# Two-layer graph kernel on one core: two transposes moved from TensorE to transposing DMA transfers

## The reference, cut to what matters

```python
h = relu(layernorm(x))
q, k, v = h @ Wq + bq, h @ Wk + bk, h @ Wv + bv
a = q @ k.T / sqrt(512)
a = a * adj + (1 - adj) * -1e6          # adj[src, dst] = 1 for each edge
x = x + softmax(a) @ v                  # x1 in the kernel
h = relu(layernorm(x))                  # h2
h = agg(h @ W1 + b1)                    # agg: product with the edge counts, scaled by dinv on both sides
h = relu(gamma * (h - mean) * rsqrt(var + eps) + beta)   # over the nodes
return x + agg(h @ W2 + b2)
```

## Time and profile before

| | before |
|---|---|
| median of 3 runs | 340.11 us (339.83 to 340.81) |
| the profiled execution's own time | 340.02 us |
| its span, first to last instruction | 338.2 us |
| PE busy | 320.2 us, 95% |
| DVE busy | 200.9 us, 59% |
| ACT busy | 112.9 us, 33% |
| POOL busy | 54.6 us, 16% |
| granted TensorE clock, mean | 1.00 |

### The profile page before, as it was taken

How to read it: one execution, slowest core, us unless ns; L and a number is a source line. 1 busy time by engine, 2 the same in 40 slices (tenths; PEclk the granted TensorE clock), 3 DMA queues, 4 the chain that set the end, 5 groups by cost and what they waited for, 6 DMA issues and landing times.

```text
span 338.2 us, 4827 instructions
## 1 busy us (share of the span) xinstructions
PE 320.2 (95%) x1466; PEld 247.5 (73%) x1466; DVE 200.9 (59%) x456; ACT 112.9 (33%) x183; POOL 54.6 (16%) x96
## 2 busy tenths in 40 slices
PE   1898889999999999899999999999999999999996
PEld 0776456777666687788888888888778887887884
DVE  5889999986869514346263636446541257559221
ACT  1909123443464412422342322232621205514000
POOL 5113000000000081512306150120101014300000
PEclk9999999999999999999999999999999999999999
DMA  7912100000230060140202030000000000000041
GB/s 217 320 39 64 62 0 1 3 0 23 102 125 0 2 124 0 36 151 1 64 1 62 2 93 0 2 0 0 0 3 0 0 2 1 2 0 0 28 150 73
DMA packets 17477, 14.83 MB, mean 44 GB/s; under 512 B 11184, under 2 KB 11440, under 8 KB 17456
## 3 DMA queue, kind: packets, MB, share of 16 engines
q1 hardware_dynamic: 17456, 14.56, 14.4%
HBM read 10.36 MB, written 2.10 MB: 37 GB/s over the span
## 4 chain that ended last, share of the span: by engine, by line
PE 78%; DVE 10%; ACT 5%; issue 3%; DVEq 1%; POOL 1%; DMA 1%; SPq 0%; ACTq 0%; POOLq 0%
PE ps L787 17%; PE ps L789 16%; PE ps L788 16%; PE ps L1065 9%; PE ps L850 8%; PE ps L984 5%; PE ps L868 3%; PE ps L927 2%; DVE src_oh L606 2%; PE ps L816 1%; ACT cnt L458 1%; PE ps L948 1%; DMA edge_i<-src_in 1%; DVE bnst L756 1%; DVE g L753 1%
## 5 line engine op out<-in xcount | busy, mean ns | idle before, releaser
L606 DVE TENSOR_SCALAR src_oh<-iota,ecol 128x512 f16 x172 | 48.9, 349 | 1.7 <-PE ps L850 0.9
L850 PE MATMUL ps<-src_oh,dst_oh 128*128 x172 | 41.2, 381 | 2.0 <-DVE dst_oh L608 2.0
L389 ACT ACTIVATE cnt<-ps 64x512 int16<-64x512 f32 x32 | 18.9, 591 | 37.8 <-PE ps L855 37.4
L850 PEld LDWEIGHTS ps<-src_oh,dst_oh 128*128 x172 | 18.3, 114 | 17.8 <-issue 5.5
L984 PE MATMUL ps<-cnt,qh 128*128 128x512 f32 x128 | 30.1, 391 | 0.2 <-ACT cnt L458 0.2
L1065 PE MATMUL ps<-qh,cnt 128*128 128x512 f32 x128 | 29.3, 390 | 0.0
L984 PEld LDWEIGHTS ps<-cnt,qh 128*128 128x128 f32 x128 | 23.9, 188 | 5.5 <-issue 0.6
L1065 PEld LDWEIGHTS ps<-qh,cnt 128*128 128x128 f32 x128 | 23.9, 188 | 5.2 <-DVE vb L768 0.3
L787 PE MATMUL ps<-v,pT 128*128 128x512 f32 x64 | 25.0, 391 | 1.0 <-DVE pT L667 1.0
L787 PE MATMUL ps<-kT,qh 128*128 128x512 f32 x64 | 25.4, 397 | 0.0
L686 DVE TENSOR_TENSOR hnT<-ps,hnT 128x512 fp32r<-128x512 f32 x8 | 5.5, 692 | 33.2 <-ACT hnT L450 33.2
(11 more groups left out here) (150 smaller groups left out, 614.0 us busy)
## 6 DMA issues: line engine op xcount, KB each, us to landing
xt<-x_in SPq DMA_DIRECT2D x16, 256.0 KB, 3.1
out<-xt SPq DMA_DIRECT2D x8, 256.0 KB, 2.0
wA_raw<-L_gnn_Wk_in SPq DMA_DIRECT2D x2, 512.0 KB, 6.6
wB_raw<-L_gnn_Wv_in SPq DMA_DIRECT2D x2, 512.0 KB, 8.1
wA_raw<-L_gnn_Wq_in SPq DMA_DIRECT2D x2, 512.0 KB, 3.7
wB_raw<-L_gnn_W_in SPq DMA_DIRECT2D x2, 512.0 KB, 3.8
w_raw<-L_gnn_W_in SPq DMA_DIRECT2D x2, 512.0 KB, 3.8
bias_row<-L_gnn_b_in SPq DMA_DIRECT2D x2, 256.0 KB, 3.7
```

The source lines that it names most:

```text
L389: act.activation(cnt16[rows, a * KC:(a + 1) * KC, w // 2, :], ps[a * WIN:(a + 1) * WIN, i % 2, :].rearrange("p (s n) -> p s n", n=P), ACT. ...
L606: dve.tensor_scalar(src_oh[:, bass.ds(slot, 1), j, :].rearrange("p a n -> p (a n)"), iota[:, :], ecol[:, bass.ds(c + j, 1)], None, ALU.is_ ...
L850: m = pe.matmul(ps[:, i % 2, :], dst_oh[:, bass.ds(slot, 1), :, j].rearrange("p a n -> p (a n)"), src_oh[:, bass.ds(slot, 1), j, :].rearra ...
```

## The change

P and h2 are no longer turned on PE. ACT scales the values by a power of two and writes the rounded fp16 value (plane 0), DVE writes the fp16 rest (plane 1), SP issues one transposing DMA for each plane, and ACT and DVE turn the landed planes back into the fp32r pair. PSUM banks 5 and 6 are free of P; `weighted_v` uses bank 4. pT, p16 and h16 have one buffer each. `ADJ` falls from 4 to 2, so `turn_counts(t+2)` waits for mask t.

The orders change with it: on PE `weighted_v(i-1)` stands ahead of `times_w1(i-2)`, also at the tail; on DVE `mask_and_max(0)` stands ahead of the query split and `large_flag`; on SP all transfers of the pipeline stand in one loop.

```diff
-ADJ = 4
+ADJ = 2
+P_UNIT = 32768.0
+H_UNIT = 2048.0
@@ SP
+        def turn_p(t, part, split, done, landed):
+            sp.wait_ge(S[split], t + 1)
+            if t >= 1:
+                sp.wait_ge(S[done], t)
+            sp.dma_start_transpose(p16T[:, part, :, :], p16[:, part, :]).then_inc(S[landed], 16)
...
-        sp.wait_ge(S["item_ps"], len(items))
-        load_w(4)
-        for t in range(XT, NT):
-            load_x(NT + t)
-            if t >= 4:
-                turn_counts(t)
+        for t in range(NT + 2):
+            if t < NT:
+                turn_p(t, 0, "p16_hi", "p_hi", "p16_hi_in")
+                turn_p(t, 1, "p16_lo", "p_lo", "p16_lo_in")
+            if 1 <= t <= NT:
+                turn_h2(t - 1, 0, "h16_hi", "h2T_hi", "h16_hi_in")
+                turn_h2(t - 1, 1, "h16_lo", "h2T_lo", "h16_lo_in")
+            if t == 0:
+                sp.wait_ge(S["item_ps"], len(items))
+                load_w(4)
+            if t + ADJ < NT:
+                turn_counts(t + ADJ)
+            if XT <= t + 3 < NT:
+                load_x(NT + t + 3)
@@ POOL, mask_fill(t)
-                pool.wait_ge(S["pT_ps"], t - 1)
+                pool.wait_ge(S["p16_lo"], t - 1)
@@ ACT
+        def p16_hi(t):
+            act.wait_ge(S["exp_done"], t + 1)
+            if t >= 1:
+                act.wait_ge(S["p16_hi_in"], 16 * t)
+            act.activation(p16[:, 0, :], T[:, t % 2, :], ACT.Copy, scale=P_UNIT).then_inc(S["p16_hi"], 1)
         def p_hi(t):
-            act.wait_ge(S["pT_ps"], t + 1)
-            if t >= 2:
-                act.wait_ge(S["pv_ps"], t - 1)
-            act.activation(pT[:, t % 2, 0, :, :], ps[:, 4:6, :].rearrange("p a (k n) -> p (a k) n", n=P),
-                           ACT.Copy).then_inc(S["p_hi"], 1)
+            act.wait_ge(S["p16_hi_in"], 16 * (t + 1))
+            if t >= 1:
+                act.wait_ge(S["pv_ps"], t)
+            act.activation(pT[:, 0, :, :], p16T[:, 0, :, :], ACT.Copy, scale=1.0 / P_UNIT).then_inc(S["p_hi"], 1)
...
+        for i in range(NT + 3):
+            if 2 <= i <= NT + 1:
                 h2_relu(i - 2)
+                h16_hi(i - 2)
+            if 2 <= i <= NT:
+                p_hi(i - 1)
+            if i >= 3:
+                h1_hi(i - 3)
+            if 2 <= i <= NT + 1:
                 h2T_hi(i - 2)
+            if i < NT:
+                softmax_exp(i)
+            if i == 1:
+                act.wait_ge(S["hT_half_used"], 1)
+                p_hi(0)
+            if i < NT:
+                p16_hi(i)
@@ DVE
+        def p16_lo(t):
+            dve.wait_ge(S["p16_hi"], t + 1)
+            if t >= 1:
+                dve.wait_ge(S["p16_lo_in"], 16 * t)
+            dve.scalar_tensor_tensor(out=p16[:, 1, :], in0=T[:, t % 2, :], scalar=P_UNIT, in1=p16[:, 0, :], op0=ALU.mult,
+                                     op1=ALU.subtract).then_inc(S["p16_lo"], 1)
             dve.wait_ge(S["exp_done"], t + 1)
             dve.reciprocal(smx[:, 3, t:t + 1], smx[:, 2, t:t + 1]).then_inc(S["rinv_ready"], 1)
...
+        for i in range(NT + 3):
+            if 2 <= i <= NT + 1:
+                h16_lo(i - 2)
+            if 2 <= i <= NT:
+                p_lo(i - 1)
+            if i >= 3:
+                h1_tmp(i - 3)
+                h1_lo(i - 3)
+            if 2 <= i <= NT + 1:
+                h2T_lo(i - 2)
             if i < NT:
                 mask_and_max(i)
                 add_loops(i)
+            if i == 0:
+                large_flag()
+            if i == 1:
+                dve.wait_ge(S["hT_half_used"], 1)
+                p_lo(0)
+            if i < NT:
+                p16_lo(i)
...
             if i == NT - 1:
 ...
             if 1 <= i <= NT:
                 residual(i - 1)
@@ PE
-                    if (n, k) == (1, KC - 1) and t >= 2:
-                        h2_turn(t - 2)
...
-            if i >= 1:
-                p_turn(i - 1)
             if i == 1:
                 make(("q", 1, 2))
                 make(("q", 1, 3))
+            if i >= 1:
+                weighted_v(i - 1)
             if i >= 2:
                 times_w1(i - 2)
-            if i >= 1:
-                weighted_v(i - 1)
...
-        early = (0, 4, 1, 5, 2, 3)
+        early = (0, 4, 1, 2, 3, 5)
         agg1((0, 1), early)
-        h2_turn(NT - 2)
-        p_turn(NT - 1)
+        weighted_v(NT - 1)
         times_w1(NT - 2)
-        weighted_v(NT - 1)
         pe.wait_ge(S["masked"], NT)
         agg1((2, 3), early)
-        h2_turn(NT - 1)
+        pe.wait_ge(S["x1_ready"], NT)
```

More of the change, by code:

```diff
@@ L148, in gnn_kernel @@
     deg_ready degm_ready degm_ps flag_ready dinv_ready
-    s_ps mask_set masked top_ready exp_done rinv_ready pT_ps p_hi p_lo pv_ps xb_ready x1_ready
-    bn_ready ln2_coef h2_ready h2T_ps h2T_hi h2T_lo w1_ps h1_tmp h1_hi h1_lo
+    s_ps mask_set masked top_ready exp_done rinv_ready p16_hi p16_lo p16_hi_in p16_lo_in p_hi p_lo pv_ps xb_ready x1_ready
+    bn_ready ln2_coef h2_ready h16_hi h16_lo h16_hi_in h16_lo_in h2T_hi h2T_lo w1_ps h1_tmp h1_hi h1_lo
     cnt_act cnt_dve bc_ps bc_ready agg1_ps g_ready g_stats z_coef z_ready z_hi z_lo
@@ L249, in _, with turn_h2 @@
         load_w(3)
+        def turn_p(t, part, split, done, landed):
[3 more added lines that the diff above has]
+            sp.dma_start_transpose(p16T[:, part, :, :], p16[:, part, :]).then_inc(S[landed], 16)
+        def turn_h2(t, part, split, done, landed):
+            sp.wait_ge(S[split], t + 1)
+            if t >= 1:
+                sp.wait_ge(S[done], t)
+            sp.dma_start_transpose(h16T[:, part, :, :], h16[:, part, :]).then_inc(S[landed], 16)
         for t in range(ADJ):
             turn_counts(t)
-        sp.wait_ge(S["item_ps"], len(items))
-        load_w(4)
-        for t in range(XT, NT):
-            load_x(NT + t)
-            if t >= 4:
-                turn_counts(t)
+        for t in range(NT + 2):
[12 more added lines that the diff above has]
+                load_x(NT + t + 3)
         sp.wait_ge(S["xb_ready"], NT)
@@ L441, in h2_relu @@
             if t >= 1:
-                act.wait_ge(S["h2T_ps"], t)
+                act.wait_ge(S["h16_lo"], t)
             act.activation(ht[:, :], x1[:, t, :], ACT.Relu, bias=lnb[:, 2, t:t + 1],
@@ L684, in h2T_lo, with h16_lo, h1_tmp, h1_lo @@
         def h2T_lo(t):
-            dve.wait_ge(S["h2T_hi"], t + 1)
-            dve.tensor_tensor(hnT[:, 1, :], bank(7), hnT[:, 0, :].bitcast(F32), ALU.subtract).then_inc(S["h2T_lo"], 1)
-        def h1_out(t):
+            dve.wait_ge(S["h16_lo_in"], 16 * (t + 1))
+            if t >= 1:
+                dve.wait_ge(S["w1_ps"], t)
+            dve.tensor_scalar(hnT[:, 1, :], h16T[:, 1, :, :].rearrange("p k n -> p (k n)"), 1.0 / H_UNIT, None,
+                              ALU.mult).then_inc(S["h2T_lo"], 1)
+        def h16_lo(t):
+            dve.wait_ge(S["h16_hi"], t + 1)
+            if t >= 1:
+                dve.wait_ge(S["h16_lo_in"], 16 * t)
+            dve.scalar_tensor_tensor(out=h16[:, 1, :], in0=ht[:, :], scalar=H_UNIT, in1=h16[:, 0, :], op0=ALU.mult,
+                                     op1=ALU.subtract).then_inc(S["h16_lo"], 1)
+        def h1_tmp(t):
             dve.wait_ge(S["w1_ps"], t + 1)
             dve.tensor_tensor(vb[:, t % 2, :], bank(7), bias_row[:, 1, :], ALU.add).then_inc(S["h1_tmp"], 1)
+        def h1_lo(t):
             dve.wait_ge(S["h1_hi"], t + 1)
@@ L712, in _ @@
                 add_loops(i)
[L713 to L714 removed]
+            if i == 0:
+                large_flag()
[4 more added lines that the diff above has]
+                p16_lo(i)
+            if i == 0:
+                lo_of(("q", 1, 1))
+            if i == 1:
+                lo_of(("q", 1, 2))
+                lo_of(("q", 1, 3))
             if i == NT - 1:
@@ L918, in scores @@
             m.then_inc(S["s_ps"], 1)
[L920 to L929, removed]
         def weighted_v(t):
+            pe.wait_ge(S["p_hi"], t + 1)
             pe.wait_ge(S["p_lo"], t + 1)
-            if t == 0:
-                pe.wait_ge(S["item_lo"], nth(("q", 1, 2)))
             if t >= 1:
@@ L937, in weighted_v @@
             for k in range(NT):
-                m = three(bank(6), lambda a: pT[:, t % 2, a, k, :], lambda a: v[:, k, a, :], k == 0, k == NT - 1)
+                m = three(bank(4), lambda a: pT[:, a, k, :], lambda a: v[:, k, a, :], k == 0, k == NT - 1)
             m.then_inc(S["pv_ps"], 1)
[L941 to L949, removed]
         def times_w1(t):
+            pe.wait_ge(S["h2T_hi"], t + 1)
             pe.wait_ge(S["h2T_lo"], t + 1)
@@ L954, in times_w1 @@
                 pe.wait_ge(S["wp_lo"], LOADS)
+                pe.wait_ge(S["item_lo"], len(items))
+            if t >= 1:
+                pe.wait_ge(S["h1_tmp"], t)
             for k in range(KC):
```

59 lines of the change are left out of this document (23 added, 36 removed).

## The result

The changed kernel takes 364.62 us (364.13 to 365.58), the kernel before beside it 339.97: a ratio of 1.072 (1.069 to 1.075), 24.6 us slower. The forecast was 360.0, slower, with 350.5 to 367.0 as its range. The span grew from 338.2 to 363.7; the profiled execution, at 365.58, is 1.0 us above the median.

What follows compares the result with a forecast made beforehand. PE bound the kernel before; afterwards loops through the other engines would. Last times_w1 17.9 us later (mask 7 alone 12.2 late), plus 1.9 for the clock, makes 19.8 on 340.02: 359.9, rounded to 360; range 350.5 to 367.

Steps and rivals of the forecast that it cites:

- SP is dearer: Rival, chance 0.13: each h2 plane's transpose holds SP 1.24 us, like one of P; 365 us in all.
- Loop L: Mask to next mask through h2's transfers, counts' transpose, x load, add_bv and fill: 19.3 us a step, setting masks 2 to 5.
- step 6: Transfer of h2's planes: 0.7 us issue on SP, 2.65 to landing, then h2T_lo on DVE 0.42.
- The new operations: ACT and DVE splits and turn-back: p16_hi 1.06 us, p16_lo 1.28, h16_hi 0.65, h16_lo 0.75, h2T_lo 0.42.
- half the new durations: Rival: p16_hi and p16_lo take 0.7 us, giving back 5: 355; inside the range, no separate chance given.
- Loop H: Mask to next mask through h2's second plane and h2T_lo on DVE: 15.0 us a step, setting masks 6 and 7.
- Mask 2: Start of tile 2's mask on DVE, put at 157.6 us against 157.32 before; the head's gain gone by then.
- Mask 7: Start of the last mask on DVE, put at 245.5 us against 233.30 before: 12.2 late.
- The tail: After mask 7: PE waits about 8 us for tile 5's h1; lower clock behind it adds 1.9, between 0 and 2.5.
- TensorE's idle time in the steps: PE idles 5.7 us ahead of weighted_v in each step with a load, 19.3 less 13.6.
- the load hidden: Rival, chance 0.07: the x load lands early enough, leaving steps of 15.0 us against 15.19; about 342.5 us.
- PE stays the bound: Faster rival, chance 0.05: mask t+1 starts within 13.6 us of mask t, steps 13.62 instead of 15.19; 328 us.

Runs made afterwards that it cites:

- 347.0: Changed kernel with the x tile's load on SP ahead of h2's two planes and the counts' transpose: 347.0 us, ratio to the kernel before 1.019.
- 345.05: Changed kernel with mask_fill ahead of add_bv on POOL, SP's order left as it was: 345.05 us, ratio to the kernel before 1.014.
- 360.5: Changed kernel with the x load ahead of the counts' transpose on SP, still behind h2's planes: 360.51 us, ratio to the kernel before 1.058.
- one-transfer run: Changed kernel with both planes of h2 turned by one 128x1024 transposing DMA instead of two of 128x512: 363.09 us, ratio to the kernel before 1.0675.
- second profile of the same kernel: Profile from running the changed kernel once more, unchanged: 364.72 us (364.28 to 365.36).
- 336.7: Changed kernel with the x load ahead of h2's planes on SP, and h1_lo and h2T_lo behind mask_and_max on DVE: 336.71 us, ratio 0.988.
- 327.0: As mended tail with the load first, but load left behind h2's planes and mask_fill ahead of add_bv on POOL: 327.03 us, ratio 0.964.
- mended tail with the load first: On top of 336.7, tile 5's h1 finished behind residual(6) between the casts, early aggregation in tile order 0 to 5: 329.99 us, ratio 0.969.

## Why the prediction was right, and where its sizes were off

The mechanism was right. The forecast of 360.0 was 4.6 us short, and the 365 of the rival "SP is dearer", to which it gave 0.13, is the nearer number.

- **PE bound before, the other engines after**: right. The chain after runs over DVE, ACT, POOL, SP and the load.
- **Loop L** (load, add, fill, mask): right in place and in number of steps, cut in two separate ways (347.0 and 345.05), and shortened by the expected link (360.5). I had 19.3 us, it takes 20.0, and 20.6 in the two steps in which the split of W2 is on POOL. The mis-sized term is step 6, the issue of h2's planes: 0.7 taken, 1.19 to 1.25 measured, so the load is issued 14.8 after the mask, not 13.9. The one-transfer run shows that the issue does not scale with the size. That rival is what happened, in most of its size: loop L grew by 0.9, where I had priced it at 1.0 to 1.1. POOL's share of the W2 split is 0.6 in two steps, not 0.2.
- **The new operations**: 1.06, 1.23 (1.28 taken), 0.63 (0.65), 0.69 (0.75), 0.43 (0.42). The rival "half the new durations" is out.
- **Loop H**: 15.0 foretold, 15.7 and 15.0 measured. The plane of h2 lands 2.5 after its issue in the median (2.65 taken), but 3.1 in the first of the two steps.
- **Mask 2** at 159.4, not 157.6: 0.66 of it was there before the pipeline (the counts' transposes start at 119.78, not 119.12), 0.3 more had been added when `weighted_v(0)` ended, and the rest, 0.8, is the issue again. **Mask 7** at 251.3, not 245.5: 1.8 from mask 2, 3.4 from three turns of loop L, 0.7 from loop H. The profiled execution is 5.7 us above the forecast for it (365.58 against 359.9), and these 5.8 are the whole of that; its median is 1.0 lower.
- **The tail**: 5.7 and 1.9 for the clock foretold, 8.0 measured. The wait for h1 of tile 5 is 7.1 us (8 foretold). The clock costs 2.5 in this profile (from the first of the 14 matmuls to `weighted_v(7)` 5.68 us, 3.18 at full clock) and 1.6 in the second profile of the same kernel (4.76); the 1.9 lay between, and which of them an execution gets was not foretold. The Trainium skill, "TensorE: Matmul & The Clock Gate", section "HAM oscillation — how this bites in real kernels", on which the prediction drew, says that an engine left idle between groups of matmuls falls back to the lower clock; the trace agrees for this wait of 7.06 us, and for the waits of 3.39 to 5.87 in the steps (granted clock 0.50 from 171 to 177, behind 5.87).
- **TensorE's idle time in the steps**: 5.7 us in each step foretold, 5.87, 3.84 and 3.90 measured under loop L and 3.39 behind it. Slower matmuls fill the difference.
- **The other rivals**: with the load hidden I had 342.5, the runs that hide it have 345 to 347, higher because loop H took 15.1 to 15.7 us a step in the better of them and not 15.0 (the chain of two of these steps passes through the split of W2 on POOL, 2.49 us, which I had put into loop L alone) and, in the other, because DVE's operations beside POOL were slower. "PE stays the bound" needs both loops cut, as the runs at 336.7 and 327.0 show.

What stays open: how much of the 2 us between the two cuts of loop L is DVE waiting on POOL. The slow operations are seen, but no run changed that alone. Open too is what decides, behind waits of 2 us and less, whether TensorE keeps its full clock; with it go some of the differences between executions of one kernel.

## What to carry to other kernels

Moving work off the busiest engine pays only up to the next loop through the others, so add up, for one step, the links from an instruction back to itself in the new order, every issue on the transfer queue among them. A transfer that other work needs early must not stand in a queue behind transfers that wait for late data: here one load had been moved behind five issues, and putting it back ahead of three of them gave back 17.6 us. The transposes do not by themselves forbid the gain: with both loops cut and the tail mended they run in a kernel 13 us faster than the one before. Where a buffer fill does not need the load, it should not stand behind it either.

## What the runs showed of the hardware that was not expected

- In the steps of the pipeline a transposing DMA held the issuing queue for 1.19 to 1.33 us whether it turned 128x512 or 128x1024 two-byte elements (up to 2.15 at about 141 to 147 us, right behind the two loads of W2). A plain load held it for 0.34 in the kernel before and for 0.57 when issued directly behind a transposing one; 0.7 us behind one it was 0.34 again (at 161.15 in the mended tail with the load first).
- A wait of 3.06 us of PE was already followed by matmuls 0.43 us apart instead of 0.227, when the kernel before had kept its full clock through 1.02 us. Between the two it went either way: 1.87 us lost the full clock in one run, 1.88 us kept it in another. And the fall can come late: in the second run of the changed kernel, behind a wait of 4.73 us, two matmuls still ran at full clock (191.69 and 192.00), and those from 192.6 to 195.2 were 0.43 apart.
- VectorE's 128x512 two-input operation on SBUF (`h16_lo`) took 0.69 us by itself and up to 1.81 with POOL's add beside it.
